# Second attention of a gated two-layer block: a unit's work put in another order on PE, DVE and ACT, and DVE's loop written out

## The reference

```python
x = x + tanh(g_xattn[0]) * L0_xattn(layernorm(x), ctx)   # 32 heads, 8 groups, keys = ctx
x = x + tanh(g_ffn[0])   * L0_ffn(layernorm(x))          # gated, inner 1376
x = x + tanh(g_xattn[1]) * L1_xattn(layernorm(x), ctx)   # the change is here
x = x + tanh(g_ffn[1])   * L1_ffn(layernorm(x))          # base matrix + 28 low-rank experts, top 2
...
# L1_xattn: q = rms_norm(xn Wq), k = rms_norm([ctx, xn] Wk), v = [ctx, xn] Wv, head size 128
# 32 query heads in 8 groups of 4 that share one k and v; softmax(q k^T / sqrt(128)) v, then Wo
```

## Time and profile before

| | us |
|---|---|
| median of 3 runs | 1468.65 |
| lowest, highest | 1466.71, 1475.12 |
| the profiled execution | 1468.23 |
| its span, first to last instruction | 1466.4 |
| second attention, first kv product of unit 0 to the tail | 534.99 to 1396.05 |

### The profile page before, as it was taken

The page is one execution under the profiler, slowest core; times in us unless marked ns, Lnnn a source line. Parts: engine busy times, 40 slices in busy tenths (PEclk is TensorE's granted clock), DMA queues, the critical chain, the costliest instruction groups (busy, mean ns, idle before and its releaser), DMA issues.

```text
span 1466.4 us, 24308 instructions
## 1 busy us (share of the span) xinstructions
PE 1393.1 (95%) x7976; PEld 1197.5 (82%) x7976; DVE 1056.6 (72%) x2794; ACT 799.1 (54%) x2210; POOL 464.6 (32%) x591
## 2 busy tenths in 40 slices
PE   4999999999999988999999999999999999999988
PEld 4899999987778877888888888888888888887777
DVE  7777777887514347787787787777787787787775
ACT  4778777773202225565555555555655655555631
POOL 3965555655937421111121111111111211112220
PEclk9999999999999999999999999999999999999999
DMA  5221111212312201001001001001001001010001
GB/s 194 73 72 60 57 70 72 72 58 72 104 42 72 98 1 72 1 1 73 1 1 72 0 1 72 0 1 72 0 1 72 0 1 72 14 42 1 1 8 51
DMA packets 14959, 63.96 MB, mean 44 GB/s; under 512 B 1761, under 2 KB 1761, under 8 KB 10657
## 3 DMA queue, kind: packets, MB, share of 16 engines
q1 hardware_dynamic: 14880, 63.07, 12.3%
HBM read 60.97 MB, written 2.10 MB: 43 GB/s over the span
## 4 chain that ended last, share of the span: by engine, by line
PE 40%; DVE 15%; issue 5%; ACT 4%; DVEq 0%; ACTq 0%
PE psum L57 12%; PE psum L59 11%; PE psum L58 11%; PE psum L1359 2%; PE psum L1453 2%; DVE mx L1044 2%; DVE pT_hi L1017 2%; DVE w1o_lo L1006 1%; DVE pT_lo L1013 1%; DVE p L1059 1%; DVE w1q_lo L1006 1%; ACT pT_hi L1215 1%; DVE dump L1037 1%; DVE oT_lo L1023 1%; DVE v_lo L1074 1%
## 5 line engine op out<-in xcount | busy, mean ns | idle before, releaser
L1292 ACT ACTIVATE p<-psum,nb,rq 128x320 f32<-128x320 f32 x256 | 155.1, 613 | 163.1 <-DVE nb L1048 163.0
L57 PE MATMUL psum<-w1q_hi,xnT_lo 128*128 128x512 f32 x288 | 121.9, 423 | 16.4 <-DVE v_lo L1068 8.6
L981 POOL TENSOR_TENSOR rk<-ssk,rms_eps 128x3 f32<-128x3 f32 x32 | 6.3, 196 | 352.1 <-DVE ssk L1085 352.1
L1013 DVE TENSOR_TENSOR pT_lo<-psum,pT_hi 128x512 fp32r<-128x512 f32 x128 | 88.1, 689 | 40.0 <-ACT pT_hi L1215 38.3
L59 PE MATMUL psum<-w1q_hi,xnT_hi 128*128 128x512 f32 x288 | 114.5, 398 | 0.0
L58 PE MATMUL psum<-w1q_lo,xnT_hi 128*128 128x512 f32 x288 | 113.7, 395 | 0.0
L1044 DVE TENSOR_REDUCE mx<-psum 128x2 f32<-128x640 f32 x128 | 105.0, 820 | 6.5 <-PE psum L59 0.9
L1256 ACT ACTIVATE q_raw<-psum 128x512 f32<-128x512 f32 x64 | 38.2, 597 | 122.7 <-PE psum L59 122.7
L57 PE MATMUL psum<-w1o_hi,oT_lo 128*128 128x512 f32 x256 | 100.5, 393 | 0.0
L58 PE MATMUL psum<-w1o_lo,oT_hi 128*128 128x512 f32 x256 | 100.3, 392 | 0.0
L59 PE MATMUL psum<-w1o_hi,oT_hi 128*128 128x512 f32 x256 | 99.8, 390 | 0.0
(11 more groups left out here) (236 smaller groups left out, 4658.3 us busy)
## 6 DMA issues: line engine op xcount, KB each, us to landing
raw_q<-in_w0q SPq DMA_DIRECT2D x8, 1024.0 KB, 4.9
raw_o<-in_w0o SPq DMA_DIRECT2D x8, 1024.0 KB, 4.8
raw_q<-in_w1q SPq DMA_DIRECT2D x8, 1024.0 KB, 7.5
raw_o<-in_w1o SPq DMA_DIRECT2D x8, 1024.0 KB, 4.8
raw_kv<-in_w_gu SPq DMA_DIRECT2D x10, 512.0 KB, 3.6
raw_gu<-in_w_gu SPq DMA_DIRECT2D x10, 512.0 KB, 3.6
raw_kv<-in_w0kv SPq DMA_DIRECT2D x8, 515.0 KB, 3.3
raw_kv<-in_w1kv SPq DMA_DIRECT2D x8, 512.0 KB, 5.5
```

Source lines behind the costliest of these rows:

```text
L57: pe.matmul(out, w[1], m[0], start=start, stop=False)
L1013: last = dve.tensor_tensor(k.pT[1][:, kt, 2 * hp:2 * hp + 2, :], bank.rearrange("p (h q) -> p h q", h=2), f(k.pT[0][:, kt, 2 * hp:2 * hp + ...
L1292: last = act.activation(k.p1[:, tile, h, :], s_pair(j)[:, h % 2, :], ACT.Exp, bias=k.nb[:, i:i + 1], scale=k.rq[:, i:i + 1], accum_out=k.r ...
```

## The change

The second attention does the same arithmetic in another order.

- q is projected by pairs of heads, not by token tiles: `q_proj` for a pair computes both tiles, 24 products with 256 columns, so 48 in a unit. `qT`, `stat` and `PAIRS` follow this: scores 0 and 1 belong to head pair 0, scores 2 and 3 to pair 1.
- On PE a unit is now: kv, cx, pv 0, turns 3 and 4 of the unit before, q pair 0, k's transposes, turn 5, q pair 1, q's transposes pair 0, pv 1, q's transposes pair 1, scores 0 and 1, out 0, scores 2, out 1, scores 3, and turns 0, 1 and 2 of this unit itself. The banks are dealt out for this order, and each user waits for the low part of the one before it in its bank; for turn 2 that is turn 0.
- DVE and ACT get orders of their own to match. On DVE the unit ends with row maximum 2, both additions to x, the scaling of p for j = 2, row maximum 3, the low parts of turns 0, 1 and 2, and the scaling for j = 3. ACT copies turns 0 to 2 in front of the last pair of exponentials.
- The weight pieces (`pieces`): o for this group in b = 1, kv and q for the next group in b = 3, the low parts of q's last two pieces on DVE at the start of the next group.
- DVE's program is written out for all eight groups; PE, ACT and POOL keep their loop.
- The tail and the layer-norm tiles in units 0, 30 and 31 are fitted to this.

u is the unit before (n - 1). The diff, cut to its core:

```diff
-    PAIRS = [(0, 0), (0, 1), (1, 0), (1, 1)]
+    PAIRS = [(0, 0), (1, 0), (0, 1), (1, 1)]
...
-        order = ["kv"] + (["cx"] if b % 2 == 0 else []) + ["q0", "q1", "pv0", "pv1", "d0", "d1"]
+        order = ["kv"] + (["cx"] if b % 2 == 0 else []) + ["pv0", "q0", "q1", "pv1", "d0", "d1"]
         name = kind if kind in ("kv", "cx") else f"{kind}{j}"
-        return by[(y_start(b) + order.index(name)) % 2]
...
-        at = {"t": j, "k": 6, "q": 7 + j}[kind]
-        return bx[(9 * b + at) % 2]
+
+        order = ["t3", "t4", "k", "t5", "q0", "q1", "t0", "t1", "t2"]
+        name = kind if kind == "k" else f"{kind}{j}"
+        return bx[(9 * b + order.index(name)) % 2]
...
+    def pieces(g, b):
+
+        return {1: [("o", g, i) for i in range(CONV["o"])],
+                3: [("kv", g + 1, i) for i in range(CONV["kv"])] + [("q", g + 1, i) for i in range(CONV["q"])]}.get(b, [])
...
+                    if b == 0 and not first:
+                        w_lo("q", g, 2)
+                        w_lo("q", g, 3)
...
-                    if prev:
-                        t_lo(n, b, 0)
-                    if b == 1:
-                        w_lo("o", g, 2)
-                        w_lo("o", g, 3)
...
+                    if prev:
+                        t_lo(u, b, 3)
+                        t_lo(u, b, 4)
+                    dve.wait_ge(rk_ready, n + 1)
+                    for i in range(nk):
+                        last = dve.tensor_scalar(k.k_raw[:, i, :], k.k_raw[:, i, :], k.rk[:, i:i + 1], None, ALU.mult)
+                    last.then_inc(k_scaled, 1)
+                    if prev:
+                        pv_lo(u, b, 0)
...
-                    if prev:
-                        t_lo(n, b, 1)
-                    dve.wait_ge(rk_ready, n + 1)
-                    for i in range(nk):
-                        last = dve.tensor_scalar(k.k_raw[:, i, :], k.k_raw[:, i, :], k.rk[:, i:i + 1], None, ALU.mult)
-                    last.then_inc(k_scaled, 1)
-                    if prev:
-                        t_lo(n, b, 2)
-                        t_lo(n, b, 3)
-                    q_squares(n, b, 0)
-                    if prev:
-                        t_lo(n, b, 4)
-                        t_lo(n, b, 5)
-                    q_squares(n, b, 1)
-                    if prev:
-                        pv_lo(n, b, 0)
+                    if conv:
+                        w_lo(*conv[0])
...
-                    for tile in range(2):
-                        dve.wait_ge(qt_hi, 2 * n + tile + 1)
-                        dve.tensor_tensor(k.qT[1][:, tile, :, :],
-                                          x_bank(b, "q", tile)[:, :].rearrange("p (h q) -> p h q", h=GH),
-                                          f(k.qT[0][:, tile, :, :]), ALU.subtract).then_inc(qt_split, 1)
-                        if prev and tile == 0:
-                            pv_lo(n, b, 1)
-                    split_next = b == BATCH - 1
+                    if prev:
+                        t_lo(u, b, 5)
+                    q_squares(n, 0)
+                    if conv:
+                        w_lo(*conv[1])
+                    q_squares(n, 1)
+                    q_lo(n, b, 0)
+                    for c in conv[2:4]:
+                        w_lo(*c)
+                    if prev:
+                        pv_lo(u, b, 1)
+                    q_lo(n, b, 1)
                     row_max(n, 0)
                     row_max(n, 1)
-                    if split_next:
-                        w_lo("kv", g + 1, 0)
                     scale_p(n, 0)
-                    if split_next:
-                        w_lo("kv", g + 1, 1)
+                    scale_p(n, 1)
+                    row_max(n, 2)
                     if prev:
-                        x_add(n, b, 0)
+                        x_add(u, b, 0)
+                        x_add(u, b, 1)
+                    scale_p(n, 2)
+                    row_max(n, 3)
+                    t_lo(n, b, 0)
+                    t_lo(n, b, 1)
                     for i, tile in enumerate(ln_tiles(n)):
                         ln.dve_lo(dve, *tile, ln_bank(b, i))
-                    if split_next:
-                        w_lo("q", g + 1, 0)
-                    row_max(n, 2)
-                    scale_p(n, 1)
-                    if split_next:
-                        w_lo("q", g + 1, 1)
-                    if prev:
-                        x_add(n, b, 1)
-                    if split_next:
-                        w_lo("q", g + 1, 2)
-                    row_max(n, 3)
-                    scale_p(n, 2)
-                    if split_next:
-                        w_lo("q", g + 1, 3)
-                    if b == 0:
-                        w_lo("o", g, 0)
-                        w_lo("o", g, 1)
+                    t_lo(n, b, 2)
                     scale_p(n, 3)

             def tail(n):
+                u = n - 1
+                w_lo("q", NKV, 2)
+                w_lo("q", NKV, 3)
...
-            loop(dve, body, tail)
+            for g in range(NKV):
+                body(g, g == 0, g < NKV - 1)
+            tail(NKV * BATCH)
...
-                    for j in range(6):
-                        if prev:
-                            t_evac(n, b, j)
-                            if j == 5:
-                                pv_evac(n, b, 0)
-                        if split_next and j in (2, 4):
-                            w_hi("kv", g + 1, j // 2 - 1)
-                        if j in (1, 3):
-                            act.wait_ge(q_full, 2 * n + j // 2 + 1)
-                            act.activation(k.q_raw[:, j // 2, :], y_bank(b, "q", j // 2)[:, :], ACT.Copy)\
-                               .then_inc(q_copied, 1)
+                    if prev:
+                        t_evac(u, b, 3)
+                        t_evac(u, b, 4)
+                        pv_evac(u, b, 0)
+                    if b == 1 and not first:
+                        act.wait_ge(d_full, 2 * u)
+                    if conv:
+                        w_hi(*conv[0])
+                    q_copy(n, b, 0)
...
-                    if split_next:
-                        w_hi("q", g + 1, 0)
-                    for tile in range(2):
-                        act.wait_ge(qt_full, 2 * n + tile + 1)
-                        act.activation(k.qT[0][:, tile, :, :],
-                                       x_bank(b, "q", tile)[:, :].rearrange("p (h q) -> p h q", h=GH),
-                                       ACT.Copy).then_inc(qt_hi, 1)
-                        if prev and tile == 0:
-                            pv_evac(n, b, 1)
-                        if tile == 0:
-                            for late in ln_tiles(n):
-                                ln.act_norm(act, *late)
-                    if split_next:
-                        w_hi("q", g + 1, 1)
-                    for j, (tile, hp) in enumerate(PAIRS):
-                        if split_next and j == 2:
-                            w_hi("q", g + 1, 2)
-                            w_hi("q", g + 1, 3)
-                        if b == 0 and j == 3:
-                            if not first:
-                                act.wait_ge(d_full, 2 * n)
-                            for i in range(CONV["o"]):
-                                w_hi("o", g, i)
...
+                    if prev:
+                        t_evac(u, b, 5)
+                    if conv:
+                        w_hi(*conv[1])
+                    for late in ln_tiles(n):
+                        ln.act_norm(act, *late)
+                    q_copy(n, b, 1)
+                    q_hi(n, b, 0)
+                    for c in conv[2:4]:
+                        w_hi(*c)
+                    if prev:
+                        pv_evac(u, b, 1)
+                    q_hi(n, b, 1)
+                    exps(n, 0)
+                    exps(n, 1)
+                    for c in conv[4:]:
+                        w_hi(*c)
+                    exps(n, 2)
+                    t_evac(n, b, 0)
+                    t_evac(n, b, 1)
+                    for i, tile in enumerate(ln_tiles(n)):
+                        ln.act_hi(act, *tile, ln_bank(b, i))
+                    t_evac(n, b, 2)
+                    exps(n, 3)
...
+                elif j >= 2:
+                    pe.wait_ge(t_split, 6 * u + (1, 2, 3, 5)[j - 2])
...
+            def out(u, b, j):
                 for h in range(GH):
+                    if j == 0 and h % 2 == 0:
+                        pe.wait_ge(pv_split, 2 * u + h // 2 + 1)
                     last = mm3(pe, y_bank(b, "d", j)[:, :], [w[:, h, j * PART:(j + 1) * PART] for w in k.oT],
                                [w[:, h, :] for w in k.w_o], h == 0, h == GH - 1)
                 last.then_inc(d_full, 1)
...
+            def q_proj(n, b, hp):
+                for tile in range(2):
+                    t = 2 * b + tile
+                    for c in range(CH):
```

(79 more changed lines are left out.)

193 lines of the change are left out of this document (94 added, 99 removed).

## The result

| | before | after |
|---|---|---|
| median, us | 1468.18 | 1490.71 (1489.31 to 1492.11) |
| ratio, 95% interval | 1 | 1.0146 [1.0117, 1.0175] |
| span of the profiled execution, us | 1466.4 | 1488.0 |

The change makes the kernel 22.5 us slower; 8.9 were forecast. The direction and the range held, the size did not. The two spans differ by 21.6 us; the medians are of runs taken side by side.

What follows compares the result with a forecast made beforehand. PE, busy 95% of the span, was taken as the bound. Looped groups +8.0, group 1 +2.7, group 0 +3.4, group 7 +1.0 and tail -6.2 gave +8.9 on 1468.2: 1477.1 us, range 1456 to 1494.

Steps and rivals of the forecast that it cites:

- The new wait: PE at turn 2, until turn 0's low half is subtracted and its bank free: 1.67 us in every unit.
- Unit lengths: Second attention, start to start with the new wait: odd units 26.4 us, even units 28.05 us.
- The stall-free length: A unit's PE work without waits: 24.7 us odd, 26.2 even, plus a 0.1 wait in even units.
- DVE written out: Group starts: DVE's jump back and its 2.40 us gap vanish, worth 1.1 us each, five times, 5.5 us.
- The q cut: q projection as 48 products of 256 columns for 24 of 512: +0.26 us per unit on PE, not hidden.
- The tail: After the second attention: q pieces split in time and three turns done already, -6.2 us, bounds -8 and -2.
- Rivals C and D: Wait behind turn 1: C, at its floor of 1.08, 1458 us, chance 0.13; D, no wait, 1424 us, chance 0.05.
- Rival B: More DVE waits, since margins of 0.3 are thin: 0.4 us more per unit, +13, 1490 us; chance 0.14.
- rival A: Standing drops PE's clock in a third of the units at 1.5 us each: +16, 1493 us; chance 0.08.
- group 0: Unit 0's turns and norms as one chain, +5.5, less 1.6 for kT_lo; +3.4 with unit 1, bounds 0 and +8.
- PE's jump: PE's loop jump, covered by the waiting turn before it; uncovered at most 2.4 us five times; nothing summed.
- Group 7: Longer chains and late norms in units 30 and 31, against old waits: +1 us, bounds -3 and +5.

Runs made afterwards that it cites:

- a_cover: Changed kernel with turns 0 and 1 moved into the middle of output product 1, ahead of scores 3; 1435.64 us, ratio 0.9786.
- b_unroll: Kernel before the change with only DVE's program of the second attention written out for all eight groups; 1459.56 us, ratio 0.9942.
- a_short: Changed kernel with DVE doing row maximum 3 and the low halves of turns 0 and 1 ahead of the second addition to x; 1474.0 us, ratio 1.0046.
- a_peout: Changed kernel with PE's group loop written out as well; 1487.48 us, ratio 1.0144.
- c_late: a_cover with turn 2 of the three layer-norm units (0, 30, 31) moved behind PE's next product; 1437.12 us, ratio 0.9792.
- the four edits there: The unit 0 edits of the changed kernel: a_unit0, a_k0, a_late0 and a_undo0; 1490.18, 1491.28, 1491.83 and 1492.93 us.
- a_loop: Changed kernel with DVE's group loop put back as a loop; 1497.31 us, ratio 1.0204.
- a_unit0: Changed kernel with unit 0's two q products in the two free banks; 1490.18 us, ratio 1.016.
- a_late0: Changed kernel with unit 0's last turns (0, 1, layer-norm turns, 2) on PE behind the kv product of unit 1; 1491.83 us, ratio 1.016.
- a_k0: a_unit0 with unit 0's second q product also ahead of k's transposes; 1491.28 us, ratio 1.0161.
- a_undo0: Changed kernel with unit 0 in its old order on PE, DVE and ACT, its turns 0 to 2 behind unit 1's kv; 1492.93 us, ratio 1.0171.

## Why the prediction was right or wrong

*Right, by its own steps.* The new wait: 1.67 us forecast, 1.65 measured, from the same chain of instructions (3.34 against 3.33 us from the start of scores 3), and covering it took 55 us out (a_cover). Unit lengths: 26.4 and 28.05 forecast, 26.45 and 28.16 measured. The stall-free length: 24.7 and 26.2 + 0.1, against 24.84 and 26.62 in a_cover. DVE written out: 1.1 at each group start in b_unroll, and no fetch cost of the longer program. The kT_lo and v_lo waits went, and none came at scores 0 or q1 in steady units. The q cut: +0.26 forecast, +0.23 measured as work. The tail: -6.2, -6.7. Rivals C and D fell: the wait is not at its floor. It could be put there, though (a_short: 1.21), and removed by moving two turns, which asked for neither a third bank nor an earlier last maximum. D's premise was too narrow. Rival B's time, 1490, came out, but not its mechanism: further waits of 0.4 us in each unit would show in the unit lengths, which are 0.04 to 0.11 over the forecast. That the measured time lies in the range is therefore luck: the range reached up there for rival A, the clock.

*Mis-sized: group 0*, +3.4 forecast, +9.1 measured, outside its bounds (0 to +8) and the largest error. The step that failed is its sum of waits in unit 0, +5.5 less 1.6, so +3.9; unit 0 grew by 8.0. The rows of the changed kernel in the last section and these of the kernel before (the windows give busy times, then the granted clock) take it apart:

```profile
549.47 0.70 PE L1453 MATMUL psum<-ident,q_raw 128*128 128x128 f32 x4 [1.92 <-DVE kT_lo L1116]
```

```profile
534.99:539.26 4.27, 4.27 (x24) 4.27 (x25) 3.52 (x2) 0.00 (x0) 0.11 (x2) 0.65 0.00 0
550.06:553.37 3.31, 3.31 (x14) 3.30 (x14) 1.68 (x3) 0.80 (x2) 0.80 (x1) 0.51 0.00 0
```

The dependent chain at the end was sized fairly: 7.5 us from the end of the scores to the end of the unit, in place of 1.3 of norm turns, so +6.2 for +5.5. The credit of 1.6 did not come: the wait of 1.92 for kT_lo went, and waits of 1.00 and 0.92 came at the next two steps, q's second transposes and the scores. Two waits were in no term: 2.69 for the context's v_lo ahead of the first q projection, since in unit 0 no value product and no turns stand between (the prediction took 0.1 for every even unit), and 1.74 ahead of scores 2 (0.22 before). Against that, kv and the first two scores were at the lower clock before and were not after, which gave back 2.6. That sums to 8.0 with 0.2 for the q cut. Unit 0 is a fill, in which every chain (context and k, q, softmax) stands open. Unit 1 was 1.4 longer than the 26.4 of the sum, of which 1.3 is its kv at the lower clock behind the 3.56 us wait; that was in no term either.

*Missed: PE's jump.* I wrote that the wait of the turn covers it. It does the reverse: 0.4 us in each of units 7, 11, 15, 19 and 23 (a_peout), with unit 27 some 1.7 us in groups 2 to 6. My bound of 2.4 us each held the size but the sum took nothing. Nor is it so that PE shows no such gap in the kernel before: it stands 1.28 us with "issue" as releaser at 561.27, ahead of the first turns of unit 1, once; the changed kernel has no such stand there, and no run shows its cause.

*Small sums.* Odd units are 0.04 and even ones 0.11 longer than forecast, 1.5 us over groups 2 to 6, and one fall of the clock is 1.5 us (below). With PE's jump that is 4.7 us, for the 4.6 by which these groups exceed the forecast.

*Group 7*, +1.0 forecast, +2.6 measured, within its bounds. Turns, norms and turn 2 run as one chain in units 30 and 31, as in unit 0. It was not taken apart further than c_late does.

*Open.* Which of unit 0's waits an edit could really take out was not settled: the medians of the four edits there lie within 2.3 us of the changed kernel, and the lower clock costs their traces some three to four microseconds in units 0 and 1, at places that differ. Why the clock falls in unit 0 in one trace and not in the next is open too.

## What to carry to other kernels

When an order is spread so that the last step of a unit reuses the bank of one just before it, the wait that appears there is paid in every unit. Walk the chain that frees the bank, and put one product between; here moving two groups of transposes half an output product forward turned +1.5% into -2.1%. At the first unit of a pipeline sum nothing from waits removed: ask what work is left over the whole chain, and bound it by the whole. And before a trace is said to show that an edit won nothing, compare the clock of the same products in both traces.

## What the runs showed of the hardware

A loop's jump back costs very different times, by what stands ahead of it: 2.33 to 2.50 us on DVE at the nine group starts where it shows, in both orders (before, a_loop), 0.4 us on PE where its queue had just stood for 1.0 (a_short) or 1.4 us, and nothing that shows on PE where it had not (a_cover).

The clock fell once in the steady stretch of the changed kernel, 4.4 us of kv in unit 16 instead of 2.95. The rows around it, and the windows (busy time of each engine, then the granted clock):

```profile
976.41 0.44 PE L1352 MATMUL psum<-ident,p 128*128 128x128 f32 x2 [1.42 <-DVE pT_lo L1016]
977.00 0.38 PE L57 MATMUL psum<-w_kv_hi,xnT_lo 128*128 128x256 f32 x1 [0.15 <-issue]
```

```profile
973.00:977.00 4.00, 2.43 (x18) 1.92 (x17) 3.62 (x9) 1.90 (x7) 0.00 (x0) 1.00 0.00 0
977.00:981.50 4.50, 4.50 (x25) 4.50 (x26) 1.69 (x5) 1.96 (x6) 0.00 (x0) 0.62 0.00 2
```

The fall to the lower level comes while PE is fully busy, right after it had stood twice. The six kernels that have both the 1.42 us wait and PE's jump (the changed one, a_unit0, a_loop, a_late0, a_k0, a_undo0) each show exactly one such fall in steady units, in one trace each, always in the first unit of a group (units 16, 20, 20, 24, 16, 24), and it costs 1.5 us (in a_loop it is hidden: unit 20 takes 29.73 us there, as other group starts do). a_peout, without the jump, a_short, with the shorter wait, and all kernels built on a_cover show none. So rival A of the prediction exists, but at a tenth of the rate that it supposed: one unit in 32 for a third of them.
